# Attention, top-1 mixture of eight experts: picks at the end of a step, gelu two tiles back, two copies of the up-product, ranks and late table placed otherwise

## The reference

```python
x = x + attention(q=layernorm(x), k=v=ctx)      # kp = ctx Wk^T, vp = ctx Wv^T + bv, softmax, then Wo, bo
xn = layernorm(x)
idx = argmax(softmax(xn @ Wg + bg))             # one expert of E = 8 for each token
h = gelu(xn @ W1[idx] + b1[idx])                # 512 -> 512, exact gelu
x = x + h @ W2[idx] + b2[idx]
```

## Time and profile before

| what | value |
|---|---|
| median of 3 runs | 469.86 us (468.12 to 474.94) |
| the profiled execution's own time | 464.87 us |
| its span | 463.1 us |
| granted TensorE clock, mean | 0.969 |
| busy share of the span: TensorE, VectorE, ScalarE, GpSimd | 88%, 69%, 57%, 51% |

### The profile page before, as it was taken

The page is one execution under the profiler, slowest core; times in us unless marked ns, Lnnn a source line. Parts: engine busy times, 40 slices in busy tenths (PEclk is TensorE's granted clock), DMA queues, the critical chain, the costliest instruction groups (busy, mean ns, idle before and its releaser), DMA issues.

```text
span 463.1 us, 8767 instructions
## 1 busy us (share of the span) xinstructions
PE 408.6 (88%) x2035; PEld 223.8 (48%) x2036; DVE 320.4 (69%) x655; ACT 263.7 (57%) x568; POOL 235.2 (51%) x305
## 2 busy tenths in 40 slices
PE   6989999997998888977869699999899989999870
PEld 2566655566776666753324244444344434444330
DVE  0286758895685777687796767777877777887640
ACT  1341109578896877944535765566656555665740
POOL 4006909101266777656783245555555665666730
PEclk9999999999998999978998899999999999999996
DMA  8999799807344496427885668787777777888520
GB/s 272 239 395 401 252 406 396 312 0 264 103 139 137 145 305 211 161 66 186 255 256 180 199 179 258 228 246 209 228 227 227 228 228 240 240 236 246 162 71 0
DMA packets 77961, 101.11 MB, mean 218 GB/s; under 512 B 9057, under 2 KB 49005, under 8 KB 76134
## 3 DMA queue, kind: packets, MB, share of 16 engines
q1 hardware_dynamic: 69646, 80.74, 57.9%
q0 software_dynamic: 6400, 19.65, 11.4%
q10 hardware_dynamic: 1880, 0.31, 0.4%
HBM read 70.80 MB, written 31.28 MB: 220 GB/s over the span
## 4 chain that ended last, share of the span: by engine, by line
PE 24%; DMA 19%; DVE 19%; issue 10%; ACT 10%; SPq 9%; POOL 4%; ACTq 2%; DVEq 0%; POOLq 0%
DMA work<-hidden_blocks 10%; SPq L536 5%; DVE work L1220 4%; PE bank L1524 4%; DMA hidden_blocks<-work 4%; ACT work L904 3%; PE bank L1311 3%; PE bank L1366 3%; PE bank L1475 3%; POOL routed_rows L683 3%; DVE expert_weights L1007 3%; PE bank L1459 2%; DMA expert_weights<-in_x 2%; PE bank L1527 2%; ACT expert_weights L767 2%
## 5 line engine op out<-in xcount | busy, mean ns | idle before, releaser
L904 ACT ACTIVATE work<-work,b_columns 128x128 f32<-128x128 f32 x136 | 59.8, 512 | 67.8 <-DVE work L1220 67.8
L1524 PE MATMUL bank<-expert_weights 128*128 x312 | 74.7, 383 | 11.4 <-DVE expert_weights L1151 4.6
L720 POOL DMA_INDIRECT out_x<-keys_values_then_rows_b x39 | 40.2, 1032 | 83.8 <-DVE keys_values_then_rows_b L1231 73.9
L1524 PE MATMUL bank<-expert_weights,ey_bias_split_then_geluT 128*128 x312 | 76.0, 387 | 7.0 <-DVE ey_bias_split_then_geluT L1225 6.9
L1220 DVE STREAM_TRANSPOSE work<-work 128x512 f32<-128x512 f32 x37 | 41.0, 1109 | 37.2 <-DMA work<-hidden_blocks 37.1
L1524 PEld LDWEIGHTS bank<-expert_weights 128*128 128x128 f16 x312 | 30.6, 98 | 52.0 <-issue 21.0
L1524 PEld LDWEIGHTS bank<-expert_weights,ey_bias_split_then_geluT 128*128 128x128 f16 x312 | 30.8, 99 | 45.8 <-issue 12.9
L683 POOL DMA_INDIRECT routed_rows<-work,slot_index x32 | 33.5, 1046 | 32.6 <-DVE slot_index L1096 25.3
L767 ACT ACTIVATE expert_weights<-expert_weights 128x512 f16<-128x512 f32 x56 | 33.9, 624 | 25.7 <-DVE expert_weights L1007 19.7
L714 POOL TENSOR_TENSOR keys_values_then_rows_b<-keys_values_then_rows_b 128x512 f32<-128x512 f32 x31 | 40.8, 1315 | 7.7 <-POOL keys_values_then_rows_b L706 7.7
L1527 PE MATMUL bank<-expert_weights,ey_bias_split_then_geluT 128*128 x156 | 41.3, 388 | 0.0
(11 more groups left out here) (200 smaller groups left out, 739.7 us busy)
## 6 DMA issues: line engine op xcount, KB each, us to landing
expert_weights<-in_L_ffn_W SPq DMA_DIRECT2D x14, 1024.0 KB, 10.3
keys_values_then_rows_b<-routed_rows SPq DMA_DIRECT2D x39, 258.0 KB, 3.3
hidden_blocks<-work SPq DMA_DIRECT2D x39, 256.0 KB, 2.6
work<-hidden_blocks SPq DMA_DIRECT2D x37, 256.0 KB, 3.1
...
```

Source lines behind the costliest of these rows:

```text
L720: pool.indirect_dma_start(out_rows, ids_of, rrow[t.buf][:, 0:D], None, bounds_check=T - 1, oob_is_err=False).then_inc(out_sent[t.buf], 16)
L904: nc.scalar.activation(gel_of(t)[:, P * c:P * (c + 1)].rearrange("p (j a) -> p j a", a=C), hid_turned[:, P * c:P * (c + 1)].rearrange("p ( ...
L1524: mm(o, a[:, c, :], w_split[:, bass.ds(first + (2 * c + h) * D, D)], start=(c == 0 and h == 0 and not begun), stop=False)
```

## The change

1. In attention, `pick_experts` stands at the end of VectorE's step, behind `pT` and `mixed`, and no longer ahead of them.
2. `copy_hidden` has two buffers (`hid[0]`, `hid[1]`), and waits for the write of the tile two back. The second is the former `gel`.
3. ScalarE's step is `copy_hidden(t)`, `gelu(t-2)`, `g_high(t-2)`, `x2_high(t+2)`. Gelu writes in place. `h_turn` writes each row in the order of tokens, every fourth number at a time, so that gelu reads and writes neighbours; before, gelu read every 32nd number and `h_turn` wrote neighbours. `h_turn(t)` therefore waits for `g_low(t-1)`, no longer for the gelu of t-1.
4. Between the stages: `x2_turn(3)`, `x2_low(4)`, `x2_high(3)` stand earlier; TensorE has `up(4)` ahead of the last `rank` and `down(0)` ahead of the count for the late table (L1593 before); VectorE does `g_low(1)`, `x2_low(5)`, `h_turn(2)`, `x2_turn(6)` inside the late table, behind its sums; SyncE issues `load_hidden(4)` ahead of its wait for the late table; ScalarE's wait for that table stands ahead of `copy_hidden(5)`, and no longer ahead of `copy_bias(0)`.

The counts of matmuls, DMAs and element operations stay as they are.

```diff
-        hid, hid_turned = (work[:, rest + D * n:rest + D * (n + 1)] for n in (1, 3))
+        hid = [work[:, rest + D:rest + 2 * D], work[:, D:2 * D]]
+        hid_early = kv[:, b2_at + 4 * D:b2_at + 5 * D]
+        hid_turned = work[:, rest + 3 * D:rest + 4 * D]
-        gel_late, gel_early = work[:, D:2 * D], kv[:, b2_at + 4 * D:b2_at + 5 * D]
...
+        def hid_of(t):
+            return hid_early if t.half and isinstance(t.j, int) and t.j < NE - 3 else hid[t.half]
...
                 if isinstance(t.j, int) and t.j == NE - 4:
+                    load_hidden(t)
                     late_ready()
...
             def copy_hidden(t):
                 act.wait_ge(h_done, t.j + 1)
-                if isinstance(t.j, int) and t.j > 0 or not isinstance(t.j, int):
-                    act.wait_ge(hw_in[(t - 1).half], 16 * (t - 1).pair + 16)
-                nc.scalar.activation(hid, bank[UP_BANK[t.half]][:, :], ACT.Copy, scale=1.0 / WSCALE).then_inc(hc_done, 1)
+                if isinstance(t.j, int) and t.j == 1:
+                    act.wait_ge(pv_done, G * ((b2_at + 5 * D - 1) // (2 * D) + 1))
+                need(act, hw_in[t.half], 16 * t.pair)
+                nc.scalar.activation(hid_of(t), bank[UP_BANK[t.half]][:, :], ACT.Copy, scale=1.0 / WSCALE).then_inc(hc_done, 1)
...
                 for c in range(C):
-                    nc.scalar.activation(gel_of(t)[:, P * c:P * (c + 1)].rearrange("p (j a) -> p j a", a=C),
-                                         hid_turned[:, P * c:P * (c + 1)].rearrange("p (a j) -> p j a", a=C), ACT.Gelu,
+                    nc.scalar.activation(hid_turned[:, P * c:P * (c + 1)], hid_turned[:, P * c:P * (c + 1)], ACT.Gelu,
...
             def step_of(t):
+                if isinstance(t.j, int) and t.j == NE - 3:
+                    act.wait_ge(tabled, 4)
+                    for u in range(U):
+                        act.wait_ge(sent[u], 16 * NTURN)
                 if t.real:
                     copy_hidden(t)
+                if (t - 2).real:
+                    gelu(t - 2)
+                    g_high(t - 2)
                 if (t + 2).real:
                     x2_high(t + 2)
-                if (t - 1).real:
-                    gelu(t - 1)
-                    g_high(t - 1)
...
-                if j % G == 0 and is_tile(k - 8):
-                    pick_experts(c, 2 * turn + (j - 8) // G, (j - 8) // G % 2)
                 if is_tile(k - 2):
                     pT(k - 2, (j - 2) % U)
                 if is_tile(k - 3):
                     mixed(c, k - 3, (j - 3) % U, turn if j >= 3 else turn - 1)
+                if j % G == 0 and is_tile(k - 8):
+                    pick_experts(c, 2 * turn + (j - 8) // G, (j - 8) // G % 2)
...
             def h_turn(t):
                 dve.wait_ge(hl_in[t.half], 16 * t.pair + 16)
-                need(dve, g_done, C * t.j)
-                nc.vector.transpose(hid_turned.rearrange("p (c a j) -> p a c j", c=C, a=C),
+                need(dve, gl_done, t.j)
+                nc.vector.transpose(hid_turned.rearrange("p (c j a) -> p a c j", c=C, a=C),
...
+            x2_turn(Slot(3))
             step(c, NT + 2, 2, NTURN)
-            x2_turn(Slot(3))
             x2_low(Slot(3))
             x2_turn(Slot(4))
             h_turn(Slot(0))
+            x2_low(Slot(4))
             step(c, NT + 4, 4, NTURN)
-            x2_low(Slot(4))
...
             summed(cum)
-
+            g_low(Slot(1))
+            x2_low(Slot(5))
+            h_turn(Slot(2))
+            x2_turn(Slot(6))
...
-            step(Slot(3))
             each_step(dve, step, 4, NJ + 4)
...
             last4 = early_experts(C, C)
+            up_early(4, last4)
             rank(2 * NTURN - 1, 1)
-            up_early(4, last4)
+            pe.wait_ge(x1_done, 2 * NT)
+            down_early(0, first4)
             pe.wait_ge(pairs_counted, 1)
             mm(ends, ones_h[:, :], seen[:, 0, :], start=True, stop=True).then_inc(counted, 1)
-            pe.wait_ge(x1_done, 2 * NT)
-            down_early(0, first4)
             down_early(1, first4)
```

26 lines of the change are left out of this document (8 added, 18 removed).

## The result

The changed kernel took 446.96 us (median of 4 runs, 444.4 to 449.57), the kernel before 468.99 us (4 runs, 465.53 to 474.94): ratio 0.955, 95% interval 0.945 to 0.965. The forecast was 454, and 443 to 467 the range. It is faster, and somewhat faster than the sum said.

The account below looks back on a forecast made before the run. A ring of engines was often last in the chain, although TensorE is busy 88% of the span. Gains of 7 + 5 + 2.5 + 1.5 = 16 us from 469.9 gave about 454 us, 8-in-10 range 443 to 467.

Parts of the forecast that it names:

- Part 1: Attention: the pick at the end of VectorE's step shortens GpSimd's ring and TensorE's waits, 7 us (0 to 12).
- Rival 1: Attention: the ring keeps its 14 us and TensorE waits at the rank instead; 461 us, chance 0.13.
- Part 2: Between the stages: new orders remove TensorE waits (3.3 us) and a slow-clock stretch (1.7 us); 5 us (-3 to 8).
- The wait of 3.6 for the bias row: Between the stages: TensorE's 3.6 us wait goes because load_hidden(4) no longer stands behind SyncE's wait for the table.
- The 3.0 ahead of down(2): Between the stages: TensorE waits 3.0 us there, since VectorE's g_low(2) stands behind the later end of the late table.
- rival 2: Between the stages: the late table, some 5 us later, eats the gain there; 459 us, at the bound 462; chance 0.12.
- one slow stretch: Between the stages: one run of matmuls at slow clock behind a long TensorE wait goes, about 1.7 us.
- Part 3: Expert loop: gelu two tiles back and two buffers give the hidden path three steps, 2.5 us (2.9 at most).
- The free patterns: Hidden path: the new access patterns cost nothing in the sum; gelu left at 512 ns, the turn about 1.1 us.
- rival 4: Loop: the turn gets dear; twice, 464 us (chance 0.06); from 2.7 us, 479 or more (0.07); three times, 498.
- rival 3: More than the sum: all TensorE waits at L1468 go, clock stays up, gelu shorter; 9 us more, 445, chance 0.10.
- Part 4: Tail: last copy_hidden no longer waits for gelu, but three rounds of turn, gelu, halves remain; 1.5 us (0 to 3.5).

Follow-up runs that it names:

- pick_alone: The kernel before with one edit, the pick of experts at the end of VectorE's step: 460.46 us against 468.48, ratio 0.981.
- the way back: The changed kernel with the pick put back ahead of the transposed probabilities: 453.31 us, ratio to before 0.965.
- changed_again: The changed kernel with no edit, run a second time with a second trace: 448.5 us against 468.07 for the kernel before, ratio 0.960.
- join_old: The changed kernel with the orders between the stages as before, except ScalarE's wait for the late table: 453.29 us, 0.957 of the kernel before.
- gelu_one_back: The changed kernel with gelu one tile back behind x2_high as before, both buffers and new patterns kept: 452.74 us, 0.959 of the kernel before.
- low_first: The changed kernel with g_low(0) ahead of the last placing and h_turn(1) ahead of x2_turn(5): 447.8 us, 0.956 of the kernel before.
- tail_and_low: The changed kernel with both the edits of turned_twice and low_first: 444.53 us, 0.948 of the kernel before.
- old_patterns: The changed kernel with the old turn and gelu access patterns from tile 5 on, gelu writing its own buffer: 453.89 us, 0.959 of the kernel before.
- turned_twice: The changed kernel with a second turned hidden buffer and, behind the loop, h_turn(t-1) ahead of g_low(t-2): 446.51 us, 0.955 of the kernel before.

## Why the prediction was right, point by point

**Part 1 was right in mechanism and size.** Forecast 7 us, measured 6.6 (pick_alone, by the stage) to 8 us (whole run), 6.3 for the way back. The cycle of `scale` was forecast at 12.5 us; the first four cycles of the changed kernel are 13.9, 11.8, 11.6 and 12.3 (starts at 125.44, 139.35, 151.16, 162.76, 175.10). The step from the picked experts to the slots, which was to shrink from 4.22 to some 2.2 us, takes 1.8 in the second cycle (142.90 to 144.73, changed_again). Over seven cycles the mean is 13.5 us (94.28 / 7, changed_again) where before has 14.5: the last three cycles, 14.2 to 15.3 us, gained 1.4 us together, and the 12.5 does not hold for them. Rival 1 (the ring keeps its length) is out.

**Part 2 was right in sign, 3 us too small, and its reasons were partly wrong.** Forecast 5 us, the stage gives 8.0 to 8.3. The step "The wait of 3.6 for the bias row goes, since `load_hidden(4)` no longer stands behind SyncE's wait for the table" failed: the wait is gone with the load in its old place (join_old), and 2.5 us of it are back with the load in its new place and gelu one tile back (gelu_one_back). The copies of the bias rows stand behind gelu on ScalarE, and a gelu two tiles back doesn't wait for tile 4's turn. The waits forecast ahead of down(0) and down(1) were 1.5 and 2.2 us, measured 1.40 and 2.48. The 3.0 ahead of down(2) didn't come (none, and 0.15 in changed_again): the table ended at 242.85 us, 31.2 behind up(0) for 26.6 before, so 4.6 us later as forecast, but down(2) stood behind up(5) and three bias rows and had no need of it yet. In its place 1.0 us that wasn't forecast stood ahead of up(4), for x2_low. So rival 2 had its cause right, and the cover was there. Of the 3 us that were missing 1.2 are waits (4.5 less for the 3.3 forecast) and 1.8 the clock (3.5 for 1.7): one slow stretch was counted, and the trace has two fewer, the other one at up(0). That second one is in part chance: traces with the same orders have such a stretch at up(0) or at down(1), and low_first and tail_and_low show that a lower clock and more idle time can stand for each other in this stage.

**Part 3 gave what was forecast and a good deal more that I had booked under part 2.** For the loop from down(4) to up(38) it is 3.3 to 3.6 us (165.8 against 162.2 and 162.5), forecast 2.5. The size is right, the reason only in part: with gelu's distance alone undone the loop took 161.4 us, with the one buffer's wait alone 161.0, so neither is needed by itself, with the old patterns alone 164.9, and with all three undone 167.4, TensorE then waiting eight times for x2_low (5.8 us). The forecast gave the gain to the first two and nothing to the patterns; which of them share it, and how, the runs don't separate. What the hidden path is worth between the stages, 5.4 us with the old orders (52.4 to 47.0) and 8.4 with the new (52.8 to 44.4), was in no term of its own. The free patterns were right for the turn: 1150 ns for 1109, and rival 4 (twice, or three times) is out. They were wrong for gelu, which I left at 512 ns and which came out at 390. Only rival 3 had it, for 9 us with the waits at L1468; 4 us at most is what old_patterns shows.

The price of such a step in the traces: a turn that writes 16 bytes on each time costs 41 ns in 1109, a gelu that reads 128 bytes on each time (and writes to another buffer) costs 122 in 390. The Trainium skill (SBUF — State Buffer, section "Door 1: The DMA port swizzle") has a penalty for both, which these rows bear out for the read of ScalarE and hardly for the write of VectorE.

**Part 4** was forecast at 1.5 us; from up(38) to the last down it was 16.5 before, and 16.0 and 15.1 after: 0.5 to 1.4. The three rounds one behind the other were forecast, and turned_twice, 13.8 us there, shows that they cost 1.3 to 2.2 us.

**The sum.** Forecast 7 + 5 + 2.5 + 1.5 = 16. Stages: 7.5 + 8.3 + 4.7 = 20.5 (changed_again), or 4.0 + 8.0 + 4.1 = 16.1 with the long cycle of the first trace. The forecast of 454 was 5 to 7 us high. About 1 to 2 of this is its base (469.9, where before measured 469.0, and 468.1 later); of the rest, as far as the stages tell, about 3 is part 2 and about 1 the loop. That the sum lies well inside the range is earned for part 1 and in part luck for the rest: part 2's named reason was wrong, and the loop's gain came only in part by the named way.
